# A graph network's layer 2 ending and layer 3 dense stage, run as two stages or as one

## The chip, the cores and the metric

The kernel runs on one core of a Trainium2 chip. A core has five engines that work side by side and wait for each other by semaphores: TensorE (PE, matmuls, with its weight loads shown as PEld), VectorE (DVE), ScalarE (ACT), GpSimd (POOL) and SyncE (SP, which here only issues DMAs). The metric is the device time of one execution in microseconds; lower is better.

## The reference, cut to what matters

Four layers of a graph network on 3125 nodes with 256 features each and 50000 edges. Each layer reads a normalised, rectified copy of x and adds its result to x. The change concerns the end of layer 2 (index L2 below) and the start of layer 3:

```
def _gat_conv(x, src, dst, W, att_src, att_dst, bias, heads, out_dim, concat):
    ...
    alpha = e / (den[dst] + 1e-16)
    out = jax.ops.segment_sum(alpha[:, :, None] * h[src], dst, num_segments=n)
    return out + bias
def _L2_gnn_ref(...):
    # every node is also its own neighbour
    return jax.nn.elu(_gat_conv(x, src, dst, W0, att_src0, att_dst0, b0, HEADS, HID, True))
def _gat_block(x, edge_index, edge_attr, W, W_e, att_src, att_dst, att_edge, bias, gamma, beta):
    xp = (x @ W).reshape(n, HEADS, C)
    a_src = jnp.einsum('nhc,hc->nh', xp, att_src)
    ...
    y = x + out.reshape(n, HEADS * C) + bias
h = jnp.maximum(_layernorm(x, axis=-1), 0.0)
x = x + _L2_gnn_ref(h, ...)
h = jnp.maximum(_layernorm(x, axis=-1), 0.0)
x = x + _L3_gnn_ref(h, ...)
```

## The kernel before

The 3125 nodes are 25 tiles of 125 (`NT`, `P`), one node per partition. x (`X`) and the sums of an attention (`acc`, 272 columns a node: 8 heads of 32 sums and a total of weights, then 8 columns for the node's own edge) stay in SBUF for the whole program. The program is a row of phases. Each phase writes one instruction list per engine, and an all-engine barrier (`phase`) ends it: the next phase's first instruction on any engine starts after the last one of all engines and the last stores of this phase. Within an engine the order is the order in the code; there is no scheduler. Loops over tiles go in groups of five (`U = 5`); group 0 is written out (`peeled`, and in `tapered` the last group too) and the groups between run in a hardware loop, where addresses and the counts of semaphore waits come from registers.

Around the change the phases are:

- `attend_phase` of layer 2 adds messages into `acc`; VectorE's last adds are at L1814.
- `attention_end_phase` (VectorE's part at L1950 to L1983). VectorE turns the totals into shares (L1950 to L1955, on all tiles at once). Then for each tile: sums times share (L1967, `zs`), the node's own projected row, which SP loads from `table_h` (L1934), times its share (L1971), plus the bias row (L1973), plus each other (L1974), and the lower part min(z, 0) (L1975), of which ScalarE takes the exponential (L1943). After five tiles come, five times over, max(z, 0) + exp (L1981) and x + that - 1 (L1983). TensorE has nothing in this phase.
- `dense_phase` with layer = 3. Per group VectorE takes the statistics of the five x tiles (`measure`, L964 to L974), ScalarE the square root (`root`, L1046), VectorE its reciprocal (`level`, L980 and L981). ScalarE writes the normalised rectified tile `hn` (L1062), TensorE transposes it in two halves (L1085), ScalarE copies that to SBUF (L1054), TensorE multiplies it by the weights (L1096, 272 columns), and VectorE's `finish` makes four things per tile: `base` (L1001), the node scores (L1002) and the staged row (L1003, L1008), which SP stores (L1122) to the table of layer 3. ScalarE also clears `acc` for the next attention (L1050). `measure(i + 1)` stands ahead of `finish(i, 0)`, and `level(i + 1)` behind it.
- `attend_phase` of layer 3 gathers rows of that table.

All matrices are in fp32: one matmul is shown as two records in the trace, one transpose as one.

## Time and profile before

| | |
|---|---|
| median of 3 runs | 3330.68 us (3329.92 to 3333.4) |
| profiled execution | 3328.81 us, its span 3327.0 us |
| busy over the span | PE 2562.3, DVE 2325.5, ACT 1696.8, POOL 1537.8 us |
| mean granted TensorE clock | 0.858 |
| from VectorE's first instruction of `attention_end_phase` to its last of `dense_phase` 3 | 2509.83 to 2636.99 us |

The profile is of one execution. Its page gives busy time per engine over the whole span, which mixes phases with different limits; for a change in one place, the rows of that place count. In the timeline each row is a start, a duration, engine, line, operation, and in square brackets the idle time of that engine before it and what ended that. An instruction that doesn't depend on the one before it starts before that one has ended, so the distance between two starts, not the duration, is what an instruction costs its engine.

### The profile page before, as it was taken

To read this page: it belongs to the slowest core of one execution; us is meant where nothing else is said; L and a number is where in the kernel's file an instruction comes from. 1 tells how busy PE (TensorE), PEld (TensorE's weight loads), DVE (VectorE), ACT (ScalarE), POOL (GpSimd) and SP (SyncE) were. 2 spreads that over 40 slices of the span, in tenths; PEclk is the share of its full clock that TensorE was granted. 3 is DMA by queue.
4 is the path that set the end of the run, shared out by engine and by line. 5 is a ranking of instruction groups with operands and counts; after the bars stand their busy time and mean duration, and the time that the engine had idled before them with its cause. 6 is when DMAs were issued, how large, how long until landed. Compare 5 with 4: busy or idle time off the path is not lost. (4 is left out here: it accounts for less than half of the span.)

```text
span 3327.0 us, 57408 instructions
## 1 busy us (share of the span) xinstructions
PE 2562.3 (77%) x13060; PEld 1934.9 (58%) x13061; DVE 2325.5 (70%) x5871; ACT 1696.8 (51%) x4048; POOL 1537.8 (46%) x1759
## 2 busy tenths in 40 slices
PE   2999998367999999999996458888870568888870
PEld 1888887234666666666664356666660356666650
DVE  4788887574777777877775637776778556666677
ACT  1666665122444555545553356666661456666651
POOL 1333332103344555545551077777750177777740
PEclk9999999688999999999997768777886768787785
DMA  2100000214455565555651155555532255555521
GB/s 69 22 9 10 8 10 7 64 63 149 124 151 152 155 163 156 153 151 156 162 154 40 47 155 139 137 138 138 137 93 38 81 145 143 144 142 142 141 68 39
DMA packets 186289, 348.95 MB, mean 105 GB/s; under 512 B 74085, under 2 KB 116478, under 8 KB 185951
## 3 DMA queue, kind: packets, MB, share of 16 engines
q0 software_dynamic: 83520, 249.39, 29.6%
q1 hardware_dynamic: 102685, 98.62, 10.3%
q8 instruction: 30, 0.49, 0.1%
q14 instruction: 54, 0.44, 0.0%
HBM read 325.45 MB, written 22.44 MB: 105 GB/s over the span
## 5 line engine op out<-in xcount | busy, mean ns | idle before, releaser
L1678 POOL DMA_INDIRECT t_rows<-table_h,t_istage x896 | 852.7, 952 | 266.1 <-issue 246.4
L1264 POOL DMA_INDIRECT b_rows<-table_kv,b_istage x448 | 481.2, 1074 | 394.0 <-PE b_pso L1401 271.1
L1765 PE MATMUL t_pso<-t_rows,t_hot 125*125 125x272 f32 (+1 forms) x1792 | 601.3, 492 | 72.7 <-DVE t_rows L1804 35.4
L1765 PEld LDWEIGHTS t_pso<-t_rows,t_hot 125*125 125x125 f32 x1792 | 404.5, 237 | 171.4 <-issue 74.5
L1326 ACT COPY b_asked<-b_psq 125x512 f32<-125x512 f32 x224 | 131.3, 586 | 475.2 <-PE b_psq L1365 475.2
L1804 DVE TENSOR_TENSOR t_rows<-t_rows,t_psm 125x1056 f32<-125x1056 f32 x224 | 276.8, 1236 | 33.1 <-issue 32.9
L1751 PE MATMUL t_pss<-node_scores,t_hot_t 125*125 x1792 | 272.6, 283 | 33.3 <-ACT t_hot_t L1709 30.5
L1751 PEld LDWEIGHTS t_pss<-node_scores,t_hot_t 125*125 125x125 f32 x1792 | 267.9, 230 | 48.9 <-issue 43.5
L1716 ACT ACTIVATE t_hot<-con_iota,g_dstl 125x125 f32<-125x125 f32 x896 | 280.3, 384 | 0.0
L1814 DVE TENSOR_TENSOR acc<-acc,t_pso 125x272 f32 (+1 forms) x448 | 192.8, 430 | 123.7 <-DVE acc L1814 69.0
L1365 PE MATMUL b_psq<-queries,b_hot_t 125*125 x896 | 235.1, 385 | 45.3 <-issue 27.4
L1381 PE MATMUL b_psk<-b_rows,con_ident 125*125 125x256 f32 x896 | 259.9, 414 | 0.0
L1401 PE MATMUL b_pso<-b_rows,b_hot 125*125 125x264 f32 x896 | 239.0, 412 | 23.9 <-DVE b_rows L1480 23.5
L1458 DVE TENSOR_TENSOR b_rows<-b_psk,b_asked 125x1024 f32<-125x1024 f32 x112 | 136.5, 1218 | 154.0 <-ACT b_asked L1326 154.0
L1707 ACT ACTIVATE t_hot_t<-t_places,t_minus 125x500 f32<-125x500 bf16 x224 | 156.5, 699 | 125.3 <-PE t_pss L1751 95.1
L1381 PEld LDWEIGHTS b_psk<-b_rows,con_ident 125*125 125x125 f32 x896 | 153.6, 191 | 91.5 <-issue 77.8
L1365 PEld LDWEIGHTS b_psq<-queries,b_hot_t 125*125 125x125 f32 x896 | 162.1, 189 | 76.1 <-issue 51.9
L1401 PEld LDWEIGHTS b_pso<-b_rows,b_hot 125*125 125x125 f32 x896 | 165.3, 195 | 55.7 <-issue 27.3
L1096 PE MATMUL d_pso<-wt,d_ht 128*125 128x512 f32 (+1 forms) x400 | 156.6, 534 | 35.5 <-DVE d_stage L1008 20.7
L1378 PE MATMUL b_psk<-we,b_attr 64*125 64x256 f32 x896 | 161.6, 437 | 24.3 <-DMA b_rows<-table_kv,b_istage 15.5
L1720 ACT ACTIVATE t_hot<-t_hot,con_ones 125x500 f32<-125x500 f32 x224 | 159.4, 712 | 7.3
L1709 ACT ACTIVATE t_hot_t<-t_hot_t,con_ones 125x500 f32<-125x500 f32 x224 | 159.4, 712 | 7.3
(393 smaller groups left out, 4959.9 us busy)
## 6 DMA issues: line engine op xcount, KB each, us to landing
t_places<-targets SPq DMA_DIRECT2D x56, 488.3 KB
t_rows<-table_h,t_istage POOLq DMA_INDIRECT x896, 4.7
b_attr<-in_attr_t SPq DMA_DIRECT2D x224, 62.5 KB
b_places<-targets SPq DMA_DIRECT2D x28, 488.3 KB
b_rows<-table_kv,b_istage POOLq DMA_INDIRECT x448, 3.6
table_h<-d_stage SPq DMA_DIRECT2D x50, 132.8 KB
t_flag<-flags SPq DMA_DIRECT2D x56, 62.5 KB
table_kv<-d_moved SPq DMA_DIRECT2D x25, 128.9 KB
```

Of the source, the lines that this page charges most:

```text
L1264: pool.indirect_dma_start(out=rows[:, h, s, :], out_offset=None, in_=table, in_offset=bass.IndirectOffsetOnAxis(ap=istage[:, h, s:s + 1], ...
L1365: mm = pe.matmul(ps_q[0:P, w * D:(w + 1) * D], hot_t[:, b % 2, v * PAIR + w, :], q, start=True, stop=True)
L1378: pe.matmul(to(v * PAIR + w), attr[half, b, w * P:(w + 1) * P], we[half], start=True, stop=False)
L1381: mm = pe.matmul(to(u), ident[0:P, 0:P], rows[0:P, h, b * G + u, 0:D], start=False, stop=True)
L1401: mm = pe.matmul(ps_o[0:P, at:at + MW], hot[:, h, b * G + u, :], rows[0:P, h, b * G + u, D:WIDE], start=u % PAIR == 0, stop=u % PAIR == PA ...
L1678: pool.indirect_dma_start(out=rows[:, r, s, :], out_offset=None, in_=table, in_offset=bass.IndirectOffsetOnAxis(ap=istage[:, r, s:s + 1], ...
L1709: act.activation(x, x, ACT.Relu, scale=-1.0, bias=con["ones"][0:P, 0:1]).then_inc(hot_ts, 1)
L1716: act.activation(hot[:, r, b * G + u, :], con["iota"][0:P, 0:P], ACT.Abs, scale=-1.0, bias=g["dstl"][:, bass.ds(n * G + u, 1)]).then_inc(d ...
L1751: mm = pe.matmul(expanded[:, b * G + u], hot_t[:, b % 2, u, :], ntab[:, bass.ds(ts[u // PAIR], 1), 0:nw].rearrange("p a d -> p (a d)"), st ...
L1765: mm = pe.matmul(ps_o[b % 2][0:P, at:at + mw], hot[:, r, b * G + u, :], rows[0:P, r, b * G + u, 0:mw], start=u % PAIR == 0, stop=u % PAIR ...
L1804: dve.tensor_tensor(v, v, weight[:, b * G:(b + 1) * G].unsqueeze(3).to_broadcast([P, G, H, HW]), ALU.mult).then_inc(mset, 1)
L1814: dve.tensor_tensor(row, row, ps_o[b % 2][0:P, v * 512:v * 512 + mw], ALU.add).then_inc(added, 1)
```

## The change

`attention_end_phase` and the third call of `dense_phase` go away, and one `turnover_phase` does the work of both, with one barrier less. It works in groups of five tiles, each group running through both halves, with the attention end two groups ahead of the multiplications. Per tile, three identity-like matmuls on TensorE add up `zs`, the node's own row and the bias in PSUM (`sums`; the bias by a row of ones), in place of VectorE's L1973 and L1974. ScalarE takes relu(-z) from PSUM and then exp of its negative (`power`), in place of VectorE's L1975. `dense_phase` keeps layers 0 to 2 and is otherwise as it was.

```diff
-def attention_end_phase(nc, con, X, acc, table, bias):
+def turnover_phase(nc, con, X, acc, table, bias, ntab, weight, bias3, table3, base):
     U = 5
+    GROUPS = NT // U
+    PAIRS = -(-U // 2)
...
+        def groups(eng, body):
+            body(0)
+            with eng.Fori(1, GROUPS - 2) as i:
+                body(i)
+            body(GROUPS - 2)
+            body(GROUPS - 1)
+        def total_of(u):
+            return ps_z[u // 2][0:P, u % 2 * D:u % 2 * D + D]
...
+            def _(sp):
+                def load(g):
+                    if not (isinstance(g, int) and g == 0):
+                        sp.wait_ge(zsum, g * PAIRS)
+                    # five loads h2 <- table, loaded[u]
+                def body(i):
+                    if there(i + 2):
+                        load(i + 2)
+                    # five stores table3 <- stage, each after evac
...
+            def _(pe):
+                def sums(g):
+                    if not (isinstance(g, int) and g == 0):
+                        pe.wait_ge(risen, g * U)
+                    for u in range(U):
+                        n = g * U + u
+                        pe.wait_ge(drawn, (n + 1) * 2)
+                        pe.matmul(total_of(u), ident[0:P, 0:P], zs[:, u, :], start=True, stop=False)
+                        pe.matmul(total_of(u), ident[0:P, 0:P], h2[:, u, :], start=False, stop=False)
+                        mm = pe.matmul(total_of(u), ones[0:1, 0:P], bias[0:1, :], start=False, stop=True)
+                        if u % 2 == 1 or u == U - 1:
+                            mm.then_inc(zsum, 1)
...
+                def body(i):
+                    for u in range(U):
+                        turn(i, u)
+                        if u:
+                            multiply(i, u - 1)
+                    multiply(i, U - 1)
+                    if there(i + 2):
+                        sums(i + 2)
+                sums(0)
+                sums(1)
+                groups(pe, body)
...
+            def _(act):
+                def power(g):
+                    for u in range(U):
+                        n = g * U + u
+                        if u % 2 == 0:
+                            act.wait_ge(zsum, g * PAIRS + u // 2 + 1)
+                        act.activation(low[:, u, :], total_of(u), ACT.Relu, scale=-1.0).then_inc(lowered, 1)
+                        act.wait_ge(lowered, n + 1)
+                        act.activation(low[:, u, :], low[:, u, :], ACT.Exp, scale=-1.0).then_inc(powered, 1)
...
+                def body(i):
+                    act.wait_ge(ready, i + 1)
+                    # five times hn
+                    copied(i, 0)
+                    copied(i, 1)
+                    if there(i + 1):
+                        root(i + 1)
+                    for u in range(2, U):
+                        copied(i, u)
+                    if there(i + 2):
+                        act.wait_ge(renewed, (i + 2) * U)
+                        power(i + 2)
+                    # clear acc of group i
...
+            def _(dve):
+                def begin(g):
+                    for u in range(U):
+                        # zs = acc * inv; wait loaded[u]; h2 = h2 * ws
...
+                def measure(g):
+                    for u in range(U):
+                        if u % 2 == 0:
+                            dve.wait_ge(powered, g * U + min(u + 2, U))
+                        dve.scalar_tensor_tensor(low[:, u, :], total_of(u), 0.0, low[:, u, :], ALU.max, ALU.add).then_inc(risen, 1)
+                    for u in range(U):
+                        # x = low - 1 + x, renewed
+                    # statistics as in dense_phase, then level(g) as there
...
+                def body(i):
+                    if there(i + 1):
+                        measure(i + 1)
+                    finish(i, 0)
+                    if there(i + 1):
+                        level(i + 1)
+                    for u in range(1, U):
+                        finish(i, u)
+                    if there(i + 2):
+                        begin(i + 2)
...
-        attention_end_phase(nc, con, X, acc, t2, w["b2"])
         t3 = dram("table_h3", N, RW)
-        dense_phase(nc, con, 3, X, acc, ntab, w["l3"], D + 2 * H, w["b3"], [t3], base)
+        turnover_phase(nc, con, X, acc, t2, w["b2"], ntab, w["l3"], w["b3"], t3, base)
```

`finish` keeps its four VectorE instructions a tile, and `hn`, `turn`, `copied`, `multiply`, `root` and the clearing of `acc` are those of `dense_phase`. There are three PSUM tiles `ps_z` of two sums each, and one set of `h2`, `zs` and `low` for five tiles.

First, ScalarE's list in the hardware loop. Before, this is the loop of `dense_phase` 3 (the exponentials L1943 stand in a loop of their own, ahead of it):

```order
L1062 ACTIVATE d_hn<-x,d_nb,d_rstd 125x256
L1054 COPY d_ht<-d_pst 128x250 x2
L1045 REGISTER_ALU
L1046 ISA
L1046 ACTIVATE d_dif<-d_var 125x5
L1054 COPY d_ht<-d_pst 128x250 x2
L1053 REGISTER_ALU
L1054 COPY d_ht<-d_pst 128x250
L1050 ISA
L1050 COPY acc<-d_zeros 125x1360
```

With the change, from the same copies on (`e_low` is the lower part of z, `e_psz` the sums in PSUM, `e_dif` the group's variances):

```order
L2049 COPY e_ht<-e_pst 128x250 x2
L2044 REGISTER_ALU
L2045 ISA
L2045 ACT_TABLE_LOAD
L2045 ACTIVATE e_dif<-e_var 125x5
L2049 COPY e_ht<-e_pst 128x250 x2
...
L2037 ISA
L2038 ACTIVATE e_low<-e_psz 125x256
L2039 REGISTER_ALU
L2040 ACT_TABLE_LOAD
L2040 ACTIVATE e_low<-e_low 125x256
...
L2068 COPY acc<-e_zeros 125x1360
```

The exponentials of a group have moved between the copies and the clearing of `acc`, five with a relu ahead of each, and the loop body holds two table loads where it held none: one ahead of the square root, behind the wait for the variances (the ISA row), and one ahead of the first exponential. In the groups written out, the load for the square root stands ahead of that wait.

Second, TensorE's list in the loop. Before, in `dense_phase` 3, the body is transposes and multiplications alone, and it ends with these rows:

```order
L1085 MATMUL d_pst<-con_ident,d_hn 128x125 x2
L1096 MATMUL d_pso<-wt,d_ht 125x272 x2
L1081 REGISTER_ALU
L1085 MATMUL d_pst<-con_ident,d_hn 128x125 x2
L1096 MATMUL d_pso<-wt,d_ht 125x272 x4
```

With the change the same rows are followed by the sums of the group after next:

```order
L2006 MATMUL e_pst<-con_ident,e_hn 128x125 x2
L2015 MATMUL e_pso<-wt,e_ht 125x272 x4
L1990 ISA
L1993 ISA
L1994 MATMUL e_psz<-e_zs,con_ident 125x256
L1995 MATMUL e_psz<-e_h,con_ident 125x256
L1996 MATMUL e_psz<-row_b,con_ones 125x256
```

The last three rows come five times a group, so a group's body has 15 more matmuls of 256 columns beside its ten multiplications of 272.

## Rows read from the trace of the kernel before

**Rows 1.** Timeline, VectorE: first and last instruction of the stretch, and the next phase.

```profile
2509.83 0.48 DVE L1950 TENSOR_TENSOR e_inv<-acc 125x200 f32<-125x200 f32 x1 [1.27 <-PEq L73]
...
2636.57 0.42 DVE L1008 COPY d_stage<-d_pso 125x256 f32<-125x256 f32 x1
...
2642.77 0.15 DVE L1904 TENSOR_SCALAR t_minus<-con_part 128x1 f32<-128x1 f32 x1 [5.78 <-PEq L73]
```

**Rows 2.** Groups of instructions, 2505 to 2592 us: count, busy us, mean ns, idle before.

```profile
L1973 DVE TENSOR_TENSOR e_h<-e_h,row_b 125x256 f32<-125x256 f32 x25 | 10.6, 425 | 0.9
...
L1943 ACT ACTIVATE e_neg<-e_neg 125x256 f32<-125x256 f32 x25 | 10.4, 417 | 72.4 <-DVE e_neg L1975 72.4
...
L1975 DVE TENSOR_SCALAR e_neg<-e_zs 125x256 f32<-125x256 f32 x25 | 7.3, 294 | 0.9
```

**Rows 3.** Timeline: first products, and the loads of the second group.

```profile
2513.16 0.43 DVE L1967 TENSOR_TENSOR e_zs<-acc,e_inv 125x256 f32<-125x256 f32 x1
2513.50 0.42 DVE L1971 TENSOR_TENSOR e_h<-e_h,e_ws 125x256 f32<-125x256 f32 x1
...
2523.83 0.28 SPq L1934 DMA_DIRECT2D e_h<-table_h  x1
...
2527.76 0.42 DVE L1971 TENSOR_TENSOR e_h<-e_h,e_ws 125x256 f32<-125x256 f32 x1 [0.59 <-DMA e_h<-table_h]
```

**Rows 4.** Stretch while group 0 loads: PE, PEld, DVE, ACT, POOL, PEclk, DMA share, GB/s.

```profile
2515.00:2520.00 5.00, 0.00 (x0) 0.00 (x0) 4.76 (x14) 1.25 (x3) 0.00 (x0) 0.50 0.43 67
```

**Rows 5.** Timeline, TensorE in dense phase 3: at clock 0.50, then at 1.00.

```profile
2595.87 1.96 PE L1096 MATMUL d_pso<-wt,d_ht 128*125 128x272 f32 x4
2597.66 0.38 PE L1085 MATMUL d_pst<-con_ident,d_hn 125*128 125x125 f32 x2
...
2632.70 0.38 PE L1085 MATMUL d_pst<-con_ident,d_hn 125*128 125x125 f32 x2
...
2632.91 1.08 PE L1096 MATMUL d_pso<-wt,d_ht 128*125 128x272 f32 x4
...
2633.83 0.38 PE L1085 MATMUL d_pst<-con_ident,d_hn 125*128 125x125 f32 x2
```

**Rows 6.** Timeline, ScalarE's clearing, and the last group's start and first finish.

```profile
2599.47 1.33 ACT L1050 COPY acc<-d_zeros 125x1360 f32<-125x1360 f32 x1
...
2627.60 2.56 ACT L1062 ACTIVATE d_hn<-x,d_nb,d_rstd 125x256 f32<-125x256 f32 x5
...
2631.76 0.42 DVE L1001 TENSOR_TENSOR base<-d_hn,row_b 125x256 f32<-125x256 f32 x1 [2.80 <-PE d_pso L1096]
```

**Rows 7.** Timeline, VectorE: two instructions in a loop, statistics of a group, two finishes.

```profile
2538.32 0.42 DVE L1981 SCALAR_TENSOR_TENSOR e_zs<-e_zs,e_neg 125x256 f32<-125x256 f32 x1
2538.89 0.42 DVE L1983 SCALAR_TENSOR_TENSOR x<-e_zs,x 125x256 f32 x1
...
2590.43 1.73 DVE L964 BATCH_NORM_STATS2 d_st<-x 125x6 f32<-125x256 f32 x5
...
2593.01 0.17 DVE L974 TENSOR_SCALAR d_var<-d_var 125x5 f32<-125x5 f32 x1
...
2600.13 0.42 DVE L1001 TENSOR_TENSOR base<-d_hn,row_b 125x256 f32<-125x256 f32 x1 [0.23 <-PE d_pso L1096]
...
2601.05 0.43 DVE L1001 TENSOR_TENSOR base<-d_hn,row_b 125x256 f32<-125x256 f32 x1
```

**Rows 8.** Stretches of dense phase 3 in which the granted TensorE clock fell.

```profile
2602.00:2604.00 2.00, 0.63 (x4) 0.36 (x4) 1.74 (x7) 1.78 (x5) 0.00 (x0) 1.00 0.31 97
2604.00:2606.00 2.00, 2.00 (x8) 1.57 (x7) 1.56 (x11) 0.58 (x2) 0.00 (x0) 0.61 0.28 86
2606.00:2608.00 2.00, 2.00 (x7) 1.44 (x7) 1.04 (x7) 0.26 (x1) 0.00 (x0) 0.53 0.14 39
```

**Rows 9.** Timeline, ScalarE: a table load at work in attention 3.

```profile
2674.23 1.28 ACT L1728 ACT_TABLE_LOAD   x1
...
2675.62 0.21 ACT L1728 ACTIVATE t_fade<-t_fade 1x8 f32<-1x8 f32 x1
```

More of the change, by code:

```diff
@@ L913, in _, with dense_phase @@
                 dve.tensor_scalar(lane[:], lane[:], -BIG, None, ALU.mult).then_inc(laned, 1)
-def dense_phase(nc, con, layer, X, acc, ntab, weight, width, bias, tables, base=None, settle=False, loads=()):
+def dense_phase(nc, con, layer, X, acc, ntab, weight, width, bias, tables, settle=False, loads=()):
     U = 5
@@ new lines, in _, with turn, multiply @@
+                load(0)
+                load(1)
+                groups(sp, body)
+                for u in range(U):
+                    sp.wait_ge(stored[u], 16 * GROUPS)
+            @block.gpsimd
+            def _(pool):
+                pool.memset(zeros[:], 0.0).then_inc(empty, 1)
+                pool.wait_ge(empty, 1)
+            @block.tensor
+            def _(pe):
[10 more added lines that the diff above has]
+                            mm.then_inc(zsum, 1)
+                def turn(i, u):
+                    n = i * U + u
+                    pe.wait_ge(hset, n + 1)
+                    if u >= 2 or not isinstance(i, int) or i:
+                        pe.wait_ge(tcopied, n if u == 0 else n - 1)
+                    for a in range(2):
+                        mm = pe.transpose(ps_t[u % 2][:, a * P:(a + 1) * P], hn[:, u, a * 128:(a + 1) * 128], ident[0:P, 0:P])
+                    mm.then_inc(tset, 1)
+                def multiply(i, u):
+                    n = i * U + u
+                    pe.wait_ge(tcopied, n + 1)
+                    if u >= 3 or not isinstance(i, int) or i:
+                        pe.wait_ge(evac, n - 2 if u >= 3 else n - 1)
+                    for a in range(2):
+                        mm = pe.matmul(ps_o[u % 3][0:P, 0:WIDTH], ht[:, u, a, :], weight[:, a, :], start=(a == 0), stop=(a == 1))
+                    mm.then_inc(mmdone, 1)
@@ L1929, in body @@
                 def body(i):
                     for u in range(U):
-                        n = i * U + u
-                        if not isinstance(i, int):
-                            sp.wait_ge(done, n - U + 1)
-                        sp.dma_start(h2[:, u, :].rearrange("p (h c) -> p h c", h=H),
-                                     table[bass.ds(n * P, P), 0:MW].rearrange("p (h c) -> p h c", h=H)[:, :, 0:C]).then_inc(loaded[u], 16)
-                peeled(sp, NT // U, body)
+                        turn(i, u)
@@ L1940, in body, with root, copied @@
+                def root(g):
+                    s = bass.ds(g * U, U)
+                    act.wait_ge(spread, g + 1)
+                    act.activation(dif[:, s], var[:, s], ACT.Sqrt).then_inc(rooted, 1)
+                def copied(i, u):
+                    act.wait_ge(tset, i * U + u + 1)
+                    act.copy(ht[:, u], ps_t[u % 2][:, 0:2 * P].rearrange("p (a m) -> p a m", a=2)).then_inc(tcopied, 1)
                 def body(i):
+                    act.wait_ge(ready, i + 1)
                     for u in range(U):
-                        act.wait_ge(low, i * U + u + 1)
@@ new lines, in body @@
+                    copied(i, 0)
[7 more added lines that the diff above has]
+                        power(i + 2)
+                    act.copy(acc[:, bass.ds(i * U, U), :].rearrange("p n x -> p (n x)"), zeros[:].rearrange("p n x -> p (n x)")).then_inc(cleared, 1)
@@ L1946, in _ @@
+                power(0)
+                root(0)
+                act.wait_ge(renewed, U)
+                power(1)
+                act.wait_ge(empty, 1)
+                groups(act, body)
             @block.vector
             def _(dve):
-                c = Tally(dve, dv)
-                c.then(dve.tensor_tensor(inv[:], acc[:, :, 0:MW].rearrange("p n (h c) -> p n h c", h=H)[:, :, :, C], acc[:, :, MW:RW], ALU.add))
-                c.then(dve.tensor_scalar(alone[:], inv[:], 0.5, None, ALU.is_lt))
@@ new lines, in body @@
+                def body(i):
+                    if there(i + 1):
[7 more added lines that the diff above has]
+                        begin(i + 2)
+                t = Tally(dve, shares)
+                t.then(dve.tensor_tensor(inv[:], acc[:, :, 0:MW].rearrange("p n (h c) -> p n h c", h=H)[:, :, :, C], acc[:, :, MW:RW], ALU.add))
@@ new lines, in _ @@
+                t.then(dve.tensor_scalar(alone[:], inv[:], 0.5, None, ALU.is_lt))
+                t.up(dve.tensor_tensor(ws[:], acc[:, :, MW:RW], alone[:], ALU.add))
+                t.then(dve.scalar_tensor_tensor(inv[:], inv[:], 1e-16, alone[:], ALU.add, ALU.add))
+                t.then(dve.reciprocal(inv[:], inv[:]))
+                t.then(dve.tensor_tensor(ws[:], ws[:], inv[:], ALU.mult))
+                begin(0)
+                t.up(dve.memset(stage[:, :, 0:MW].rearrange("p u (h c) -> p u h c", h=H)[:, :, :, C:HW], 1.0))
@@ L1987, in final_phase @@
+                measure(0)
+                level(0)
+                begin(1)
+                groups(dve, body)
 def final_phase(nc, con, X, acc, base, gamma, beta, out):
```

124 lines of the change are left out of this document (80 added, 44 removed).

## The prediction

> **What bounds the kernel now.** I read the page's busy shares first, and left them: they mix all phases. The change touches one stretch, so I read the timeline of that stretch, then its groups, then the clock and the DMA by stretches. The stretch begins with VectorE's first instruction of the attention end at 2509.83 and ends with its last of dense phase 3, which starts at 2636.57 and takes 0.42: 127.2 us of the 3327.0 [rows 1]. After it come 5.78 us in which the last store lands and the barrier passes [rows 1]; that part stays. In the first phase VectorE works nearly without a gap while ScalarE idles 72.4 us waiting for it [rows 2] and TensorE does nothing. In dense phase 3 a tile's finish costs VectorE 0.92 us [rows 7] and TensorE a period of 1.13 us at full clock [rows 5], so there the two take turns. The question is what a group of five tiles costs once both halves share one loop.
>
> **What goes.** VectorE loses three instructions a tile: L1973 and L1974 at 425 ns and L1975 at 294 ns, 25 of each, 28.5 us [rows 2] if all of it were on the path. It also loses one barrier of about 1 us.
>
> **What comes, and the prices.** I price by distances between starts. An independent product of 256 columns costs VectorE 0.34 [rows 3]; where the address comes from a register and the input from the instruction before, 0.57 [rows 7], so I take 0.45 in the loop. Statistics of five tiles with the seven small instructions: 2590.43 to 2593.2, 2.75 us [rows 7]. TensorE at full clock: transposes 0.21, the two multiplications of a tile 0.92, so 0.43 for a matmul of 256 columns and 1.3 us for the three of a sum; results are out 0.17 later. At half clock the two multiplications take 1.79 (2595.87 to 2597.66), so a sum 2.6 [rows 5]. That is 6.5 us (half: 13) of new TensorE work a group. The trace has no relu from PSUM; I take for relu plus exp two times 0.42 [rows 2], 0.85 us a tile, between 0.7 if it overlaps as VectorE's do and 1.1 if each waits 0.13 more for the one before.
>
> The table loads are new too: two a group in the loop. In attention 3 one takes 1.28 and the next activation starts 1.39 after the load's start [rows 9], so I take 1.4. The Trainium skill, "ScalarE: Activation LUTs", section "What ACT_TABLE_LOAD costs", gives the same 1283 ns and adds a drain of 1380 ns for each switch to another set, 2.66 us in all. The trace shows 1.39 and no second term; by the page's figure each exposed switch would cost 1.3 us more, some 9 us over the seven exposed ones.
>
> **The sum.** T is the time from 2509.83.
>
> 1. Shares, unchanged: to T = 3.3 [rows 1, 3].
> 2. Group 0. A tile is 128 KB, and the loads run at 67 GB/s [rows 4], 1.9 us each. The first product with a loaded tile runs at 3.7 without a wait [rows 3], so the fifth tile is there at 11.3. TensorE has been idle, and the clock stands at 0.50 [rows 4], but the loads set the pace: the sums end at 13.1. ScalarE 0.85, VectorE's first pass 0.5, x five times 0.34, 2.75 for the statistics: 18.9. Square root and `level` 0.8: 19.7.
> 3. Group 1's loads are a new wait. They are released only when the sums of group 0 are done, 13.1. From issue (2523.83) to use (2527.76) took 3.9 [rows 3], and four more tiles 7.6: 24.7, and the products end at 25.2. Behind VectorE's wait stand `measure(1)` and every finish. TensorE rested 7 us and starts at half clock: sums end at 29.4. ScalarE has one table load and five pairs: 31.0. VectorE: 0.6 + 1.7 + 2.75 = 36.0. Then five finishes and `level`, 5.1: 41.1.
> 4. Three cycles, each from the start of a group's products (`begin(i + 2)`) to the end of finish(i + 1, 4). The first pair of sums is out after 0.85 + 0.1 + 2.6 + 0.2 = 3.8. ScalarE then needs five pairs and the table load, 5.65: 9.45. TensorE's other sums (6.5 in all) lie beside that, as do the loads, released at the end of the previous sums, half a cycle ahead. VectorE's first pass of the last tile, 0.6: 10.05. x five times 0.45: 12.3. Statistics, with 0.35 for registers: 15.4. Beside that ScalarE clears `acc` (1.33) and makes `hn`, and TensorE the first multiplication, which in dense phase 3 came 4.16 us after the first `hn` [rows 6]. Then the exposed table load and the root: 17.1, with finish(i, 0) beside it, and `level`: 17.7. Four finishes at 0.92 and 0.2 for TensorE: 21.6. Three cycles, the last 0.5 shorter since its square root's load stands ahead of the wait: 64.3, T = 105.4.
> 5. Group 4's finish: from the first `hn` to the last finish 9.4 (2627.60 to 2636.99) [rows 1, 6]. That `hn` waits for ScalarE's copies and clearing and so starts 0.6 before finish(3, 4) ends, and 0.8 goes to the clock: T = 115.0.
>
> That is 12.2 us under 127.2. In it are only some of the small waits between engines: each cycle has eight hand-overs that I priced at 0.05 to 0.1 or at nothing, in a loop whose semaphore counts come from registers. I put 0.7 a cycle and 0.7 each for head and tail on them, 3.5 in all. Forecast: 8.7 us saved, a profiled execution of 3320.1 against 3328.81, and against the median of 3330.68, which is 1.9 above that execution, 3322.0.
>
> So the 28.5 us of instructions removed shrink to 8.7: the group's chain now runs VectorE, TensorE, ScalarE, VectorE, and back, and only about 17 of a cycle's 21.6 us have VectorE at work.
>
> **The clock.** In the old dense phase the granted clock fell to 0.61 and 0.53 for some 3.4 us, after 2602 to 2604, where TensorE was busy 0.63 of 2 us [rows 8]. In a new cycle TensorE's sums end about 7.6 after the cycle's start and the first multiplication comes at 13.6; between lie only transposes. I expect the fall there every time, to the level of 1.2 GHz, lasting into the first two multiplications; most of it lies beside the statistics and the root, and some 0.4 us a cycle (step 4's last term) and the 0.8 of step 5 remain. Bounds from both sides: with 2.4 GHz throughout the head is 3 shorter and cycles and tail 2.3 together, and without slack that gives T = 109.7, a gain of 17.4, 3313.3. With 1.2 GHz throughout the sums let a cycle's exponentials end 5.4 later and the multiplications take 2.2 a tile: a cycle of 31, and the whole T = 158, 31 us lost, 3362.
>
> **Rivals.**
>
> A. *The small waits eat the gain.* Nothing new is wrong, but the chain's links cost more: if each register-addressed instruction costs the full 0.57 - 0.34 = 0.23 [rows 7] where I took 0.11, three groups with some 25 of them give 7 us more: 3329. For it: a chain over four engines has no cover, every hand-over counts. Against it: the old loop ran with such addresses and VectorE kept its pace (finish 0.92 [rows 7]). Time 3325 to 3334, no change. If a switch costs what the page says, it ends here as well.
>
> B. *The clock stays down during the sums.* Place: L1994 to L1996 in the loop. TensorE ends the multiplications, waits about 1.5 us for the first product and then works five sums at 2.6 instead of 1.3. They end 14.1 into the cycle, ScalarE's last pair at 14.9 instead of 9.45: 5.4 us a cycle, 16 for three, and 3 in the head and tail together, since step 3 already has half of it. Time 3322 + 19 = 3341, slower. It decides from about half of the sums at 1.2 GHz on (8.7 of 19). For it: rows 8 shows that a short rest is enough. Against: in rows 5 the clock came back within two tiles of dense work, and the rest ahead of the sums is short.
>
> C. *No fall and no slack.* The clock stays at 2.4 GHz as it did from 2608 on in the old phase, and the hand-overs hide: 3313 to 3317.
>
> That the work isn't done in the new order can be left out: the lists of the engines show it. Nor can the phases behind it gain or lose: they begin behind a barrier.
>
> **How the numbers follow.** A difference under 0.2% (6.7 us) can't be told from none. The forecast, 3318 to 3325: 45%, nine tenths of it under 3324. Rival C: 15%. Rival A: 27%, all of it within 6.7 us, as is 3% of the forecast's part. Rival B and anything else on that side: 13%. So faster 0.54, the same 0.33, slower 0.13. The range of eight in ten takes C in and B's lower half: 3313 to 3338; the likeliest case's own range is 3318 to 3325.
>
> **What would show it.** VectorE's stretch from the first share to the last staged copy ends near 118.5. A cycle of the loop is 21 to 23 us, and VectorE idles in it some 4 us for ScalarE's exponentials and 1 for the root. Group 1's products wait for their loads until about T = 25. Nine table loads of 1.28. The sums run at 0.43 a matmul, the first multiplication of a group at the half clock. Wrong would be: cycles over 24.5 us, sums of over 2 us a tile in the loop, switches of 2.6, or VectorE busy through the whole cycle.

## The result, and the profile after

| | before | after |
|---|---|---|
| median of 16 runs each, us | 3331.7 (3326.24 to 3334.24) | 3342.85 (3335.37 to 3347.89) |
| profiled execution / its span, us | 3328.81 / 3327.0 | 3346.51 / 3344.7 |
| from the shares to the last finish, us | 127.2 | 142.8 |

The ratio of after to before is 1.0035, with a 95% interval of 1.0028 to 1.0042: 11 us slower, where 9 us faster was forecast. This is rival B of the prediction, the clock that stays down during the sums. Its price of 3341 was 2 us off, but the loss lies largely in another place than it said. The profiled execution is one of 3346.51, 3.7 us above the median; the stretches below belong to it.

The stretch of [rows 1] in the timeline of after, VectorE: its start, the starts of the three cycles, the end of the last cycle, the last instruction, and the next phase.

```profile
2511.72 0.49 DVE L2148 TENSOR_TENSOR e_inv<-acc 125x200 f32<-125x200 f32 x1 [1.27 <-PEq L73]
...
2567.60 0.41 DVE L2083 TENSOR_TENSOR e_zs<-acc,e_inv 125x256 f32<-125x256 f32 x1
...
2595.61 0.41 DVE L2083 TENSOR_TENSOR e_zs<-acc,e_inv 125x256 f32 x1
...
2623.52 0.41 DVE L2083 TENSOR_TENSOR e_zs<-acc,e_inv 125x256 f32 x1
...
2645.99 0.41 DVE L2133 COPY e_stage<-e_pso 125x256 f32<-125x256 f32 x1
...
2654.06 0.41 DVE L2133 COPY e_stage<-e_pso 125x256 f32<-125x256 f32 x1
2660.07 0.15 DVE L1899 TENSOR_SCALAR t_minus<-con_part 128x1 f32<-128x1 f32 x1 [5.60 <-PEq L73]
```

The stretch is 15.6 us longer, out of 17.7 between the two spans; 1.9 more was there before it began (2511.72 against 2509.83). The head takes 55.9 us instead of the forecast 41.1, the cycles 28.0, 27.9 and 22.9 instead of 21.6, 21.6 and 21.1, the tail 8.1 instead of 9.6. So the head lost the most.

Who waited for whom stands in the groups of instructions of after, for the stretch (busy us, mean ns, then idle before and its releaser):

```profile
L1996 PE MATMUL e_psz<-row_b,con_ones 1*125 1x256 f32 x50 | 26.7, 628 | 0.0
...
L2097 DVE SCALAR_TENSOR_TENSOR e_low<-e_psz,e_low 125x256 f32<-125x256 f32 x25 | 9.7, 420 | 46.1 <-ACT e_low L2040 46.1
L2038 ACT ACTIVATE e_low<-e_psz 125x256 f32<-125x256 f32 x25 | 9.4, 377 | 73.7 <-PE e_psz L1996 73.6
L2045 ACT ACT_TABLE_LOAD x5 | 6.4, 1283 | 2.4 <-DVE e_var L2115 2.3
L2040 ACT ACT_TABLE_LOAD x4 | 5.1, 1283 | 0.1
```

VectorE waits 46.1 us for the exponentials, but ScalarE isn't the cause: it idles 73.7 us itself, for L1996, the last matmul of each sum. Read a wait through to the engine that was really late: here TensorE.

What TensorE did, in the clock of its sums. Stretches of after; the columns are those of [rows 4] (length, PE, PEld, DVE, ACT, POOL, PEclk, DMA share, GB/s). The rows are the sums of group 0, of group 1, of group 2 in two parts, of group 3 in two parts, and of group 4:

```profile
2516.40:2532.00 15.60, 15.60 (x30) 8.22 (x30) 4.56 (x13) 2.98 (x8) 0.00 (x0) 0.50 0.16 26
2539.30:2555.00 15.70, 15.68 (x30) 8.22 (x30) 4.25 (x12) 4.26 (x9) 0.00 (x0) 0.50 0.10 16
2568.50:2571.00 2.50, 2.50 (x9) 1.69 (x10) 2.50 (x8) 0.00 (x0) 0.00 (x0) 0.94 0.35 112
2571.00:2582.00 11.00, 11.00 (x22) 5.42 (x20) 1.54 (x5) 4.26 (x9) 0.00 (x0) 0.50 0.03 10
2596.00:2598.00 2.00, 1.58 (x6) 0.96 (x6) 2.00 (x8) 0.00 (x0) 0.00 (x0) 1.00 0.33 105
2598.00:2611.00 13.00, 12.75 (x25) 6.58 (x24) 2.55 (x8) 4.48 (x10) 0.00 (x0) 0.50 0.05 16
2624.00:2633.00 9.00, 8.47 (x30) 4.78 (x30) 3.97 (x12) 4.43 (x10) 0.00 (x0) 1.00 0.15 48
```

Group 0's sums and group 1's never leave the half clock (1.2 GHz), although TensorE doesn't rest once in 15.6 us. Those of groups 2 and 3 start at 2.4 GHz and fall to half some 2 us later, while TensorE works without a gap. Only the last group's run at full clock to the end. Rival B had five sums on end at half clock too, but because of a rest ahead of them; a clock that falls while the engine works without a gap was in no case of the prediction. The TensorE rows of after give the price of a tile's three matmuls as the distance from one tile's first matmul to the next tile's, first at half clock, then at full (start, length, and idle before):

```profile
2542.44 1.22 PE L1994 MATMUL e_psz<-e_zs,con_ident 125*125 125x256 f32 x2
...
2545.58 1.22 PE L1994 MATMUL e_psz<-e_zs,con_ident 125*125 125x256 f32 x2
...
2624.32 0.70 PE L1994 MATMUL e_psz<-e_zs,con_ident 125*125 125x256 f32 x2 [1.77 <-DVE e_h L2088]
...
2626.00 0.70 PE L1994 MATMUL e_psz<-e_zs,con_ident 125*125 125x256 f32 x2
```

At full clock a sum takes 1.68 us (2624.32 to 2626.00), not 1.3. At half it takes 3.14 (2542.44 to 2545.58), not 2.6, and five take 15.7.

### The profile page after: what moved, and what is told of

The parts are those of the page before. It is cut to its first block and busy times, and to the rows that moved or that the text cites. A ratio compares the mean times of both kernels' runs of the same rounds, so it can differ in the third digit from the quotient of the medians.

```text
span 3344.7 us, 57366 instructions
## 1 busy us (share of the span) xinstructions
PE 2639.6 (79%) x13210; PEld 1975.6 (59%) x13211; DVE 2293.9 (69%) x5796; ACT 1716.2 (51%) x4081; POOL 1540.9 (46%) x1759
## 5 line engine op out<-in xcount | busy, mean ns | idle before, releaser
L1376 PEld LDWEIGHTS b_psk<-b_rows,con_ident 125*125 125x125 f32 x896 | 153.2, 191 | 90.9 <-issue 77.4
L1373 PE MATMUL b_psk<-we,b_attr 64*125 64x256 f32 x896 | 160.8, 435 | 22.6 <-DMA b_rows<-table_kv,b_istage 13.3
L587 ACT COPY r_powers<-r_psn 128x256 f32<-128x256 f32 x320 | 115.0, 373 | 84.9 <-PE r_psn L626 78.1
```

Of the source, the lines that this page charges most:

```text
L1373: pe.matmul(to(v * PAIR + w), attr[half, b, w * P:(w + 1) * P], we[half], start=True, stop=False)
L1376: mm = pe.matmul(to(u), ident[0:P, 0:P], rows[0:P, h, b * G + u, 0:D], start=False, stop=True)
```

## The experiments

Two theories stood at the start. I: identity weights are nearly all zeros, so matmuls with them don't bring the clock up, whatever their number. II: it is the third matmul, whose weights and data have one row, and which uses one row of the array. A third view was that the clock needs time, and any matmuls would do. Every ratio below is against runs of the kernel before on the same chip. The runs clock_kinds, bias_all_rows, two_sums and vector_sums were made on chip A, where the kernel before takes 3638.73 us and gathers are slower, so from these only ratios and the local stretch are used. The others ran on three chips where it takes 3331.44 (chip B: two_sums_again, vector_sums_again, before_again, spread_begin), 3329.68 (chip C: after_again, bias_all_rows_again, before_folded, vector_folded) and 3329.62 us (chip D: spread_vector, spread_begin_again).

**clock_kinds.** A kernel that holds nothing of the network but ten blocks of 30 matmuls, with a rest of 13.7 us ahead of each but the first; everything else is left out. The kinds of block:

```
"a": matmul(ps, wt[:, k % 2, 16:16 + P], wt[:, (k + 1) % 2, :])   # dense weights, 128 rows, 272 columns
"b": matmul(ps, ident[0:P, 0:P], x(k))                            # identity, 256 columns
"c": matmul(ps, ones[0:1, 0:P], bias[0:1, :])                     # one row
"d": b, b, c in turn                                              # the three of a sum
"e": matmul(ps, X[:, 21 + k % 2, 0:P], x(k))                      # dense weights, 125 rows
"f": matmul(ps, ones[0:P, 0:P], x(k))                             # a full matrix of ones
ORDER = "abcdefaedb"
```

> A kernel with nothing but ten blocks of 30 matmuls in fp32, with rests of some 12 us made by VectorE between them, and x copied to the output (the rest of the computation is left out). Kinds: a is a multiplication like the dense stage's (dense weights of 128 rows, 272 columns moving), b moves x through the identity, c moves one row against one row of ones, d is b, b, c as in a sum of the changed kernel, e moves x through dense weights of 125 rows, f moves x through a full matrix of ones. Order: a b c d e f a e d b. Theory I (the identity's zeros do not raise the clock): a, e and f reach granted clock 1.00 within some 4 to 7 us, b, c and d stay at 0.50 through their whole block (30 matmuls of about 1.0 us). Theory II (the single row is what holds the clock down): a, b, e and f rise, c stays at 0.50, and d stays down or flickers. Rival (the fall has nothing to do with the kind, dense back-to-back work always rises): all ten blocks end at 1.00 and 0.43 to 0.56 us a matmul.

Stretches of its profile (length, PE, PEld, DVE, POOL, PEclk, DMA share, GB/s; this kernel has no ACT column), one of each kind, then the second block d and the second block b:

```profile
50.00:65.00 15.00, 15.00 (x59) 12.13 (x60) 0.00 (x0) 0.00 (x0) 1.00 0.00 0
80.00:95.00 15.00, 14.61 (x59) 11.98 (x58) 0.00 (x0) 0.00 (x0) 0.88 0.00 1
110.00:135.00 25.00, 24.25 (x57) 18.21 (x56) 0.19 (x1) 0.00 (x0) 0.50 0.00 0
150.00:178.00 28.00, 28.00 (x54) 14.70 (x54) 0.00 (x0) 0.00 (x0) 0.50 0.00 1
195.00:210.00 15.00, 12.90 (x57) 10.79 (x55) 1.53 (x1) 0.00 (x0) 0.95 0.00 0
225.00:240.00 15.00, 12.50 (x53) 10.33 (x52) 1.76 (x1) 0.00 (x0) 0.93 0.01 2
...
310.00:341.00 31.00, 31.00 (x60) 16.06 (x59) 0.00 (x0) 0.00 (x0) 0.50 0.00 0
355.00:370.00 15.00, 15.00 (x58) 12.57 (x59) 0.00 (x0) 0.00 (x0) 0.83 0.00 0
```

In every block whose matmuls use all rows, with identity weights (b) too, the clock reaches 1.00 (in the first block a it stood there from the start); so theory I falls. It stays at 0.50 in the block of single rows (c) and, both times, through the whole of d, where two in three are the very matmuls of b. Theory II holds, and time alone doesn't bring the clock up.

The timeline of TensorE shows what these matmuls cost at half clock: block c, and two triples of block d.

```profile
108.29 25.96 PE L146 MATMUL k_psc<-row_b,con_ones 1*125 1x256 f32 x60 [13.68 <-DVE k_rest L171]
147.92 2.07 PE L144 MATMUL k_psb<-x,con_ident 125*125 125x256 f32 x4 [13.68 <-DVE k_rest L171]
...
151.06 2.07 PE L144 MATMUL k_psb<-x,con_ident 125*125 125x256 f32 x4
```

Thirty single rows in a line take 25.96 us, 0.87 each, about what a matmul with all rows and as many columns takes at half clock (three of them take 2.56 in bias_all_rows_again below). A triple of block d takes 3.14 us (147.92 to 151.06), as in the kernel, where three times 0.87 would be 2.6. So the extra half microsecond comes with the change between the two kinds, not with the row.

**bias_all_rows.** The kernel after, with the bias added by a third matmul of 125 rows:

```diff
-mm = pe.matmul(total_of(u), ones[0:1, 0:P], bias[0:1, :], start=False, stop=True)
+mm = pe.matmul(total_of(u), ident[0:P, 0:P], bias[:, :], start=False, stop=True)
```

`bias` already holds the row in all partitions. The number of matmuls, their columns and the values of the bias are unchanged.

> The changed kernel with the bias matmul fed from all 125 partitions (identity times the bias tile, which holds the row in every partition) in place of one row of ones; same count, same columns. Theory II (the single row holds the clock down): the sums reach clock 1.00 within a group, 1.6 us a tile instead of 3.1, and the time falls to about 3325. Theory I (identity weights do not raise it): sums stay at 3.1 us a tile, 3343 within 3.

It took 3627.35, ratio 0.9968 (0.9953 to 0.9982), stretch 114.7 us. Since chip A was unlike the one of the result, it and the kernel after ran once more, together on chip C.

> The kernel after with the third matmul of a sum made from 125 rows (the identity times the bias spread over all partitions) in place of one row of ones times one row of bias: as many matmuls, as many columns. Its first run, on a chip with slower gathers, gave a stretch of 114.7 us and 0.9968. Theory (the single row keeps the granted clock at 0.50): stretch 113 to 117 us against 142.8 of the kernel after, so 26 to 30 us less than after, ratio 0.9955 to 0.997. Rival (that chip made before's gathers slow and the ratio means little; the third matmul costs its time whatever its rows): within 5 us of after, 1.002 or more.

> The kernel after, unchanged, on the same chip as the next three, for a second profile and a ratio beside theirs. Theory: the granted clock is at 0.50 through the sums of the first two groups again, a sum of a tile takes 3.1 us there, and ratio 1.003 to 1.005. If where the clock falls were chance, a second profile would show sums of group 0 or 1 at full clock.

The kernel after took 3345.17 (ratio 1.0052, 1.0035 to 1.0069; stretch 140.1), bias_all_rows 3317.61 (0.9962, 0.9945 to 0.9978; stretch 117.3). One matmul's operands make 28 us. In the second profile of the kernel after both first groups' sums stand at 0.50 again, so that isn't chance. Later groups vary: the sums of group 2 fell to half in the first tile, those of groups 3 and 4 stayed at full clock throughout. The two profiles compared; first stretches of both in after_again, then one of its group 4:

```profile
2513.77:2529.30 15.53, 15.53 (x30) 8.22 (x30) 4.58 (x13) 2.97 (x8) 0.00 (x0) 0.50 0.17 26
2536.00:2552.00 16.00, 15.31 (x30) 8.22 (x30) 4.92 (x14) 4.26 (x9) 0.00 (x0) 0.50 0.11 18
...
2618.00:2626.50 8.50, 8.25 (x30) 4.78 (x30) 3.63 (x11) 4.13 (x9) 0.00 (x0) 1.00 0.10 32
```

and TensorE's timeline in bias_all_rows_again:

```profile
2514.87 1.06 PE L1994 MATMUL e_psz<-e_zs,con_ident 125*125 125x256 f32 x2
...
2517.43 1.06 PE L1994 MATMUL e_psz<-e_zs,con_ident 125*125 125x256 f32 x2
...
2519.19 0.59 PE L1994 MATMUL e_psz<-e_zs,con_ident 125*125 125x256 f32 x2
...
2520.48 0.59 PE L1994 MATMUL e_psz<-e_zs,con_ident 125*125 125x256 f32 x2
```

The clock comes up at the third tile. A sum takes 2.56 us at half clock (2514.87 to 2517.43) and 1.29 at full (2519.19 to 2520.48): exactly the 2.6 and 1.3 of the prediction. The single row costs twice: it keeps the clock down, and among matmuls of 125 rows it stretches a sum at equal clock by 0.4 (full) to 0.6 us (half). The second goes with the change between the kinds, as clock_kinds showed; what in that change takes the time is open.

**two_sums.** The bias goes out of the stage: it is added where the table of layer 2 is evicted, in place of a copy. A node's own share and its neighbours' add up to one, so the bias on every row of the table comes out once. VectorE waits once for the bias's load ahead of that dense phase.

```diff
 # dense phase of layer 2, the eviction
-dve.tensor_copy(stage[...], o[:, 0:D]...)
+dve.tensor_tensor(stage[...], o[:, 0:D]..., bias[:]..., ALU.add)
 # the one stage
-mm = pe.matmul(total_of(u), ones[0:1, 0:P], bias[0:1, :], start=False, stop=True)
```

> The changed kernel with two matmuls a sum: the bias is added in layer 2's dense stage to the projected rows of the table (weights of an attention add up to one, so the result is the same), by the copy that stages them, now an addition at the same cost. Theory I: the clock behaves as in the changed kernel, a tile's sum takes 2.0 us at the low clock instead of 3.1, and ScalarE's last exponential of a group comes 5.7 us earlier in four groups: about 3322 to 3326. Theory II: besides, the clock rises, 1.1 us a tile: 3315. Rival (the sums are hidden and the chain around them is what counts): within 3 of 3343.

> The one stage with the bias folded into the table of layer 2, so that a sum is two matmuls with the identity and the single-row matmul is gone. Its first run was on a chip whose gathers were slower: ratio 0.9968, stretch 109.2 us. Theory (the single row keeps the granted clock at 0.50, and half clock in the sums is the loss): the stretch is 107 to 111 us again against 127.2 of before, so about 18 us less, of which the table's addition takes nothing measurable since it takes the place of a copy: ratio 0.9945 to 0.9955 on a chip where before is near 3332 us. Rival (the gain of the stretch is taken back by what comes before or after it, since the ratio of the first run was 0.9968 and not 0.995): 0.9965 or more.

On chip A 3626.01, ratio 0.9968 (0.9956 to 0.998), stretch 109.2. On chip B 3312.76: 0.9939 (0.9926 to 0.9952), stretch 110.7. The ratio there is a little better than expected, and the rival, that something outside takes the gain back, has fallen for that chip.

**vector_sums.** The one stage, but with both sums and the bias on VectorE as before (`zs += (h2 * ws + bias)`), ScalarE reading `zs`, and no `sums` on TensorE.

> The changed kernel with the sums made by VectorE again (bias and own row added in SBUF as before the change, relu and exp still on ScalarE), TensorE's three matmuls a tile gone, all else as in the changed kernel. Theory (the sums on TensorE at the low clock are the loss): VectorE pays two more instructions a tile, about 0.9 us, 4.5 a group, and the chain loses up to 15.7 us a group of sums. A cycle of the loop near 20.5 us against 28 now, the stretch near 107 us against 142.8 now and 127.2 before: 3311, faster than both. Rival (one stage in groups of five is a long chain over engines whatever makes the sums): cycles stay above 24.5 us and the time at 3335 or more.

> The one stage, with the two sums and the bias made by VectorE as before, no sum on TensorE. In its first run, on a chip whose gathers were slower, the stretch was 112.8 us and yet the ratio 1.0027. Two readings: (a) the stretch counts and the rest was noise of that chip (its runs lay 25 us apart): then here about 14 us less than before, ratio 0.995 to 0.997; (b) something outside the stretch takes it back, by some 20 us: then 1.000 or more again, and the profile shows the stretch starting later than before's.

The first run, 3646.68 and 1.0027 (1.0011 to 1.0042), went against its own stretch of 112.8 us (107 was expected). Beside bias_all_rows on the same chip, whose code outside the stretch is the same, its stretch begins 13.4 us later (2683.82 against 2670.39) and 16.4 us more come behind it; why isn't found. On chip B it took 3319.51, ratio 0.9961 (0.9947 to 0.9975), stretch 113.9: reading (a). So the kernel gains 12 us with nothing moved to TensorE. Not all of that need be the one stage's: the lower part of z stays on ScalarE here, so VectorE is also rid of L1975, 7.3 us of work [rows 2], and no run has the one stage with that instruction back on VectorE.

**before_again.** The kernel before, profiled on chip B.

> The kernel before, unchanged, for a profile on the chip on which the next three run. Its stretch from the shares of layer 2 to the last finish of the dense stage was 127.2 us in the profile of before; the same is expected within 2 us on any chip, since no gather lies in it. If it is instead some 15 us longer on a chip whose gathers are slower, the local stretches of kernels from different chips can't be compared.

3331.13 us, and its stretch is 131.0 (2507.02 to 2638.01), not within the 2 us expected. Of the 3.8 us, 3.7 lie in dense phase 3, between its first and last staged copy, in before and in before_again:

```profile
2596.19:2636.57 40.38, 32.41 (x140) 22.86 (x139) 30.74 (x142) 23.87 (x51) 0.00 (x0) 0.94 0.25 74
```

```profile
2593.51:2637.60 44.09, 36.41 (x140) 25.72 (x139) 30.77 (x143) 23.99 (x51) 0.00 (x0) 0.85 0.23 70
```

The same instructions, with the clock at 0.94 on the mean or at 0.85. A stretch is known to some 4 us from one profile, which is why the conclusions here go by the ratios.

**before_folded** and **vector_folded.** The bias folded into the table as above, in the kernel before (the addition L1973 is gone), and in vector_sums (one addition a tile).

> The kernel before with its two stages, and the bias of layer 2 added where the table of layer 2 is evicted, so the addition of 25 tiles (0.42 us, 0.46 from start to start) goes from VectorE in the stretch. It separates what folding the bias gives alone from what the one stage gives. If VectorE sets the time there: 25 x 0.46 = 11.5 us less, ratio 0.9965. Then the one stage with folded bias and sums on TensorE (18.7 us less than before) owes 11 us to the fold and 7 us to all the rest. If the gathered loads' waits take the place of the additions: under 5 us, 0.9985 or more.

> The one stage with the bias folded into the table and the sums on VectorE (one addition a tile), no sum on TensorE. Beside the kernel with two matmuls a sum it tells what moving the sums to TensorE is worth once the bias is gone. VectorE has 25 x 0.42 = 10.5 us more to do, but waits less for the exponentials (they start behind the first addition rather than behind TensorE's sums). With sums on VectorE and the bias addition the one stage gave 0.9961; less 25 x 0.43 = 10.6 us it would be 0.993 if VectorE sets the time there, better than the 0.9939 of two matmuls a sum. If its waits for TensorE and ScalarE grow instead, 0.995 or more, and the sums on TensorE are worth their place.

before_folded took 3323.34, ratio 0.9979 (0.997 to 0.9988): 6 to 7 us, not 11.5. VectorE's groups say where the rest went, in before_again (chip B) and then in before_folded (chip C, an execution of 3328.68 us, 5 above its median):

```profile
L1971 DVE TENSOR_TENSOR e_h<-e_h,e_ws 125x256 f32<-125x256 f32 x25 | 10.5, 419 | 0.7 <-DMA e_h<-table_h 0.7
```

```profile
L1980 DVE TENSOR_TENSOR e_h<-e_h,e_ws 125x256 f32<-125x256 f32 x25 | 10.6, 424 | 4.8 <-DMA e_h<-table_h 4.7
```

Four of the 11.5 us came back as waits for the loads, which the additions had hidden. From the first share to the first statistics of dense phase 3, a part that this phase's clock doesn't touch, it is 71.5 us against 77.4 in before_again, 5.9 less; so some 1.6 us more went, and aren't accounted for. vector_folded took 3305.31, ratio 0.9928 (0.9912 to 0.9945), stretch 104.2.

**spread_begin** and **spread_vector.** The order of VectorE in the loop, in two_sums and in vector_folded: the products of the group after next stand one tile at a time behind the finishes.

```diff
     level(i + 1)
+    begin(i + 2, [0])
     for u in range(1, U):
         finish(i, u)
-begin(i + 2)
+        begin(i + 2, [u])
```

> As the kernel with two matmuls a sum and the folded bias, and the products of the group after next are put one tile at a time behind the finishes of this group instead of behind all five. Then VectorE's waits for TensorE in the finishes (about 1.4 us a group) are filled, and TensorE finds the products of four tiles ready when it comes from the last multiplication: the exponentials start about 2 us earlier behind the products, so VectorE's wait for them (2.4 + 0.7 us a group) falls to about 1. Expected: cycles of 17.5 to 19 us against 20.5, over three groups 5 to 9 us less: ratio 0.002 below that of the kernel with two matmuls. Rival: the wait for the exponentials only moves, since ScalarE can't begin the next group's before it has copied the last transposed tile: under 2 us.

> The same order with the sums on TensorE as two matmuls with the identity, on the same chip; its first run gave 0.9923. If TensorE is the better place for the sums once the clock is up, it is 0.002 below the kernel with the addition on VectorE (10.5 us less work there); if not, it is level with it or above: VectorE's 10.5 us saved come back as its wait for the exponentials (11.2 us in the first run), since these start only behind TensorE's sums.

> The one stage with the bias folded into the table, one addition a tile on VectorE, no sums on TensorE, and the products and the addition of the group after next put one tile at a time behind the finishes. With all products behind the finishes this kernel gave 0.9928, with VectorE waiting 13.9 us for TensorE in the finishes and 0.1 us for the exponentials. If the spread fills those waits in the three groups that have a group after next (about 1.5 to 2.5 us each): 5 to 7 us less, 0.991. Rival (the finishes get later by the work put between them, TensorE's multiplications wait for the evictions and the next group's normalization for ScalarE): no gain, 0.9925 or more.

spread_begin took 3305.71, ratio 0.9923 (0.991 to 0.9936); its stretch of 105.7 is 5.0 shorter than that of two_sums, the lower end of what was expected. Again, beside spread_vector on chip D, 3304.61, ratio 0.992 (0.9906 to 0.9935). spread_vector took 3297.41, ratio 0.99 (0.9885 to 0.9915), stretch 97.9: the fastest, 32 us under before and, by the two ratios, some 45 under after. The two of one chip, in VectorE's groups, spread_begin_again first (an execution of 3312.03 us, 7 above its median; that of spread_vector is 2 above):

```profile
L2138 DVE TENSOR_TENSOR base<-e_hn,row_b 125x256 f32<-125x256 f32 (+1 forms) x25 | 10.6, 423 | 10.8 <-PE e_pso L2023 10.7
L2096 DVE TENSOR_TENSOR e_h<-e_h,e_ws 125x256 f32<-125x256 f32 x25 | 10.5, 420 | 5.3 <-DMA e_h<-table_h 5.3
...
L2105 DVE SCALAR_TENSOR_TENSOR e_low<-e_psz,e_low 125x256 f32<-125x256 f32 x25 | 9.5, 419 | 10.8 <-ACT e_low L2048 10.8
```

```profile
L2082 DVE TENSOR_TENSOR e_zs<-e_zs,e_h 125x256 f32<-125x256 f32 x25 | 10.6, 425 | 0.9
L2124 DVE TENSOR_TENSOR base<-e_hn,row_b 125x256 f32<-125x256 f32 (+1 forms) x25 | 10.5, 422 | 8.3 <-PE e_pso L2012 8.2
L2080 DVE TENSOR_TENSOR e_h<-e_h,e_ws 125x256 f32<-125x256 f32 x25 | 10.5, 419 | 2.0 <-DMA e_h<-table_h 2.0
L2091 DVE SCALAR_TENSOR_TENSOR e_low<-e_zs,e_low 125x256 f32<-125x256 f32 x25 | 8.8, 417 | 0.1
```

The additions on TensorE save VectorE 10.6 us of work (L2082, 25 of 425 ns) and bring it 10.7 us of waiting for the exponentials, 3.3 more for the loads and 2.5 more for TensorE in the finishes; the stretch is 104.2 against 97.9. So with the single row gone the move to TensorE still doesn't pay. That it costs is likely but not certain: the medians on chip D are 7 us apart, while the two ratios' intervals overlap a little, as do those of two_sums_again (0.9939) and vector_folded (0.9928); and with the bias in the stage the two are level (bias_all_rows_again 0.9962, vector_sums_again 0.9961). Of the change's parts, the one stage together with the relu on ScalarE pays, and the sums in PSUM don't.

## Why the prediction was wrong

- **The price and the clock of the sums** (the prices, then steps 2 to 4): this is the step that failed. "A sum 1.3 us at full clock, 2.6 at half" was taken from multiplications with 128 rows, and given to a sum with a single-row matmul in it. Measured: 1.68 and 3.14, and mostly at half clock. With 125 rows in its place (bias_all_rows_again) the forecast of the stretch, 118.5, meets 117.3, its head of 41.1 meets 43.1, and its cycles of 21.6, 21.6 and 21.1 meet 22.4, 21.4 and 20.8. Of the 3.5 us of slack, 2.3 were used. The signs of being wrong that the prediction named came: cycles over 24.5 us, and sums of over 2 us a tile in the loop.
- **Step 2**, "the loads set the pace", failed by the same term, and by the prediction's own price too: it put the clock at 0.50, where a sum was to take 2.6, more than the 1.9 of a load, and yet its 13.1 has the last sum at the 1.3 of full clock. Five sums of 2.6 from T = 4.2 on would end at 17.2. In bias_all_rows_again they end at 14.5, because the clock comes up at the third tile; that this head comes out near the forecast is in part luck. In after the sums end at T = 20.4.
- **Step 3**, "a new wait" for group 1's loads, isn't what held up after. The loads are released at T = 20.4 and the last product ends at T = 31.9, not 25.2, but TensorE has worked on group 1's sums since T = 27.6. They take 15.7 us and end at T = 43.3, not 29.4: 11.4 us behind the products, where 4.2 was priced. These 13.9 us are nearly all of the head's 14.8.
- **Step 4.** The cycles of groups 2 and 3 are 6.4 us over, the last only 1.8, since its sums are at full clock but take 0.4 a tile more. Rival B had 5.4 for each of three, and 3 for head and tail together. Measured: 14.5 for three and 13.3 for head and tail together, 24.3 over the 118.5 once the 3.5 of slack in it are taken off, where it had 19. Its stretch would have been 137.5, against 142.8 and, in after_again, 140.1. That its time was only 2 us off owes something to chance; its places were wrong.
- **Rival B's evidence.** It was argued from rests [rows 8], so it got little of the chances: "the rest ahead of the sums is short". A rest isn't enough to explain the fall: in bias_all_rows_again TensorE rests 1.76 us ahead of the sums of group 2 (1.75 in after) and these stay at 1.00. Nor does the clock need a rest to stay down: TensorE worked for 28 us in a row at 0.50 (clock_kinds, the first block d). In the Trainium skill, "TensorE: Matmul & The Clock Gate", section "Part 1: The HAM clock gate", the clock follows how busy TensorE has been; the trace agrees for matmuls of all rows and not for single rows, and there the measurement decides. The profile of before had no row of that kind, and the prediction named the matmul without giving it bounds of its own.
- **The fall in the gap** between sums and first multiplication is there, in bias_all_rows_again (three stretches from the end of group 2's sums into the first multiplication):

```profile
2556.00:2560.00 4.00, 2.15 (x10) 1.52 (x9) 2.09 (x6) 3.86 (x11) 0.00 (x0) 1.00 0.06 10
2560.00:2563.40 3.40, 0.86 (x4) 0.40 (x4) 3.12 (x10) 3.40 (x8) 0.00 (x0) 0.90 0.42 65
2563.40:2565.40 2.00, 1.98 (x5) 1.41 (x6) 1.01 (x7) 0.83 (x2) 0.00 (x0) 0.50 0.33 51
```

- **Table loads** were right. From the load's start to the activation behind it takes 1.30 us in the loop, against the 1.4 priced:

```profile
2588.49 1.28 ACT L2045 ACT_TABLE_LOAD   x1 [1.17 <-DVE e_var L2115]
2589.79 0.21 ACT L2045 ACTIVATE e_dif<-e_var  x1
```

  The drain of 1.38 us that the Trainium skill, "ScalarE: Activation LUTs", section "What ACT_TABLE_LOAD costs", adds to each switch isn't there; here the measurement decides.
- **Relu and exp** were priced a little too high, 0.85 us a tile. In ScalarE's timeline of after, a tile takes 0.74 from start to start:

```profile
2607.64 0.38 ACT L2038 ACTIVATE e_low<-e_psz 125x256 f32<-125x256 f32 x1 [3.45 <-PE e_psz L1996]
2608.06 0.42 ACT L2040 ACTIVATE e_low<-e_low 125x256 f32<-125x256 f32 x1
2608.38 0.37 ACT L2038 ACTIVATE e_low<-e_psz 125x256 f32<-125x256 f32 x1
```

- **Rival A**, that small waits cost more in a loop with register addresses, has nothing for it: a tile's two products start 0.67 apart in the loop (2595.61 and 2596.28), against the two 0.45 priced.
- **The chances** don't quite follow from their parts: nine tenths of 0.45 and C's 0.15 make 0.555 for faster, not 0.54, and A's 0.27 with the tenth that is left 0.315 for the same, not 0.33. It changes nothing in the outcome, to which 0.13 was given.

## What to carry to other kernels

Before a matmul goes into a chain that must be fast, look at how many rows it uses: a bias as one row of ones is cheap in columns and dear in clock. With the bias spread over the partitions the same kernel was 28 us faster, and folded into an earlier table it needs no matmul at all. When a wait names an engine, follow that engine's own idle time to the one that is late. And work taken from the busiest engine is gained only as far as the chain doesn't get longer by it: 10.6 us of additions moved to TensorE came back as 16.5 us of waits.

## What the runs showed of the hardware that was not expected

- Matmuls with one row of weights and one row of data, 30 in a line: the clock at 0.50 throughout 25.96 us. One such in three, between identity matmuls of 125 rows: 0.50 through 28 and 31 us of work without a gap. With identity weights, mostly zeros, alone the clock came up (blocks b: 0.88 and 0.83 on the mean of 15 us), as it did with dense ones (block e: 0.95). Changing between the two kinds took 3.14 us a triple at half clock, where three of one kind take 2.6.
- In the kernel a stretch of such sums that began at half clock never rose (groups 0 and 1, both profiles), and one that began at full clock either fell within some 2 us while TensorE worked (groups 2 and 3 of after, group 2 of after_again) or kept it (group 4 of after, groups 3 and 4 of after_again). What decides between these two stays open.
- The same phase of the same kernel differed by 3.7 us between two executions on two chips, with the clock at 0.94 and at 0.85 on the mean.
- On one of the chips the kernel before took 3638.73 us instead of some 3330. Its gathers are slower: over the same five slices of the page, in an attention phase, 110 to 116 GB/s in bias_all_rows, 137 to 141 in bias_all_rows_again. There vector_sums, whose stretch is 14 us shorter than that of before, measured 1.0027, and 0.9961 on another chip.
